# Vision tokenizer and two layers on one core: head matrices later, second norm on GpSimd, running count by products, selection and gather in halves of experts

## The reference

```
def layernorm(y):                       # everywhere, eps = 1e-5
    mu  = mean(y); var = mean((y - mu) ** 2)
    return (y - mu) * rsqrt(var + eps)
# head matrices of the latent attention
core_h = 0.5 * (core + core.T) + head_residual[h] - mean_h(head_residual)
# mixture of experts, expert chooses its tokens
score  = sigmoid(gate_w @ x)            # 8 experts x 384 tokens
top    = the 48 largest scores of each expert
y_e    = layernorm(x)[top] * gamma + beta          # gather
out_e  = fc2_e(gelu(fc1_e(y_e) + b1_e)) + b2_e
x     += scatter of score * out_e back to its tokens
```

## Time and profile before

| | |
|---|---|
| median of 3 runs | 251.8 us (251.53 to 256.31) |
| profiled execution, its own time | 249.22 us |
| its span, first to last instruction | 247.3 us |
| mean granted TensorE clock | 0.984 |
| PE busy | 228.3 us (92%), 1474 instructions |
| DVE busy | 141.3 us (57%) |
| ACT busy | 70.8 us (29%) |
| POOL busy | 63.7 us (26%) |
| fillers, L402 | 156 instructions, 40.2 us busy |

### The profile page before, as it was taken

One profiled execution on the slowest core, in us unless ns is written; L12 is line 12 of the kernel. 1 busy time (PEld: TensorE's weight loads), 2 busy tenths in 40 slices (PEclk: granted clock), 3 DMA queues, 4 the chain that ended last, 5 costly groups with the idle time before them and its releaser, 6 DMA issues.

```text
span 247.3 us, 4034 instructions
## 1 busy us (share of the span) xinstructions
PE 228.3 (92%) x1474; PEld 178.6 (72%) x1474; DVE 141.3 (57%) x401; ACT 70.8 (29%) x176; POOL 63.7 (26%) x146
## 2 busy tenths in 40 slices
PE   6999999999979987999989899999989899999994
PEld 4878788889868876787768678887668554654662
DVE  1657667565667566556665647668479835231212
ACT  2123242275575463125104310313020033120100
POOL 0179941344530150212241402021130340000000
PEclk9999999999999999999999968999999999999999
DMA  6999246920000000299999800000000004782002
GB/s 181 347 415 346 64 107 181 431 96 4 0 0 3 1 3 0 54 420 427 289 343 424 339 0 3 0 0 4 0 0 1 0 3 119 305 360 68 0 3 64
DMA packets 8772, 33.41 MB, mean 135 GB/s; under 512 B 1072, under 2 KB 2864, under 8 KB 6448
## 3 DMA queue, kind: packets, MB, share of 16 engines
q1 hardware_dynamic: 8752, 33.15, 36.7%
HBM read 32.75 MB, written 0.39 MB: 134 GB/s over the span
## 4 chain that ended last, share of the span: by engine, by line
PE 71%; DVE 13%; POOL 4%; DMA 4%; issue 3%; ACT 3%; SPq 1%; DVEq 0%; POOLq 0%
PE bank L411 11%; PE bank L945 6%; PE bank L919 6%; PE bank L642 5%; PE bank L633 5%; PE bank L535 4%; PE bank L402 3%; PE bank L560 3%; PE bank L953 3%; PE bank L513 3%; PE bank L692 2%; DMA bench<-patches 2%; PE bank L892 2%; PE bank L703 2%; PE bank L436 2%
## 5 line engine op out<-in xcount | busy, mean ns | idle before, releaser
L411 PE MATMUL bank<-desk,bench 118*126 118x256 f32 x190 | 43.2, 380 | 1.6 <-DMA desk<-conv_w 1.5
L402 PE MATMUL bank<-zeros 128*128 128x256 f32 x156 | 40.2, 400 | 1.1 <-POOL small L1867 1.1
L411 PEld LDWEIGHTS bank<-desk,bench 118*126 118x126 f32 x190 | 34.8, 188 | 6.9 <-DMA desk<-conv_w 1.9
L402 PEld LDWEIGHTS bank<-zeros 128*128 128x128 f32 x156 | 29.9, 200 | 6.3 <-POOL small L1867 1.1
L1001 DVE TENSOR_REDUCE bench<-bench 118x70 f32<-118x630 f32 x19 | 14.7, 798 | 9.0 <-DMA bench<-patches 9.0
L1637 ACT ACTIVATE attic<-bank,cols 128x126 f32<-128x126 f32 x38 | 15.2, 452 | 12.3 <-PE bank L423 12.1
L1630 ACT ACTIVATE desk<-bank 126x256 f32<-126x256 f32 x19 | 7.3, 383 | 29.1 <-PE bank L411 27.1
L1693 ACT ACTIVATE bench<-bank 128x384 f32<-128x384 f32 x8 | 3.9, 491 | 40.2 <-PE bank L626 40.2
L1874 POOL TENSOR_SCALAR small<-small 96x2 f32<-96x2 f32 (+2 forms) x15 | 3.5, 231 | 43.6 <-DVE small L1212 21.3
L642 PE MATMUL bank<-layw,bench 128*96 128x256 f32 x48 | 13.4, 428 | 1.3 <-ACT bench L1693 0.6
L633 PE MATMUL bank<-bench,layw 128*128 128x192 f32 x72 | 12.9, 332 | 1.5 <-ACT bench L1693 1.4
(11 more groups left out here) (191 smaller groups left out, 420.0 us busy)
## 6 DMA issues: line engine op xcount, KB each, us to landing
attic<-experts SPq DMA_DIRECT2D x10, 1024.0 KB, 8.6
desk<-experts SPq DMA_DIRECT2D x6, 1024.0 KB, 13.6
bench<-patches SPq DMA_DIRECT2D x19, 315.0 KB, 4.3
desk<-tokenizer_w SPq DMA_DIRECT2D x4, 576.0 KB, 6.5
layw<-layer_w SPq DMA_DIRECT2D x1, 2184.0 KB, 11.3
attic<-bias SPq DMA_DIRECT2D x8, 256.0 KB, 12.0
cons<-constants SPq DMA_DIRECT2D x1, 1130.0 KB, 5.3
desk<-conv_w SPq DMA_DIRECT2D x5, 128.0 KB, 3.2
```

The lines of the kernel that those rows point to most:

```text
L402: mm(bank[b][:, 0:C], zeros[:, 0:P], zeros[:, :], start=True, stop=True)
L411: i = mm(conv_bank[t % 2][0:TP, 0:C], xt[t % XRING][0:KP, k, :], convw[0:KP, k, :], start=(k == 0), stop=(k == KX - 1))
```

## The change

It has seven parts.

1. *DMA order at the start.* Each of the five parts of `convw` has a semaphore of its own, and `conv(0)` waits for each in turn; `load_x(1)` comes ahead of the first part of the constants; the head matrices are loaded after `load_x(6)`, and the four parts of `tokw` two tiles later. The first `keep_warm` has 4 products in place of 5.
2. *Head matrices later.* The ten `prepare_heads` stand behind the copies of tiles 5 to 14.
3. *Epsilon in the statistics.* Each statistics buffer has 9 values in place of 6; the last three are set once (24 memsets on DVE) to a third group whose spread adds epsilon to the variance. POOL's addition of epsilon goes everywhere. In `rs_and_shift` the root comes ahead of the negated mean.
4. *Gate values per group.* `halve(0)` and `halve(1)`, 192 columns each, the first ahead of `add_mixed(1)`. Values are turned right after, and ACT copies them out.
5. *Second norm on POOL.* `norm(4, g)` leaves DVE; `norm_again(g)` does it on POOL, ahead of the memset of `ysT`.
6. *Running count by products.* The marked scores are turned at once (4 transposes), the comparison is made on 96 x 32, two dependent additions form sums of whole tiles, and three products with a triangle and with ones give the slot numbers, which one multiplication masks. The scan goes. The filler ahead is 14 products in place of 24, and the fillers of 2 and 2 around the gather go.
7. *Halves.* Picks, weights, gather and the evacuation with gamma and beta run for experts 0 to 3 and then 4 to 7, into banks 2, 3 and 6, 7. POOL's weights wait for all eight half picks. `hidden(q)` waits for its half alone.

Some semaphores of the latent attention are merged, with the same order of work.

```diff
             for k in range(KX):
-                sp.dma_start(convw[:, k, :], convw_d[:, k * C:(k + 1) * C]).then_inc(s("convw_in"), 16)
+                sp.dma_start(convw[:, k, :], convw_d[:, k * C:(k + 1) * C]).then_inc(s(f"convw_in{k}"), 16)
+            load_x(1)
             sp.dma_start(cons[:, 0:CONS_NOW], cons_d[:, 0:CONS_NOW]).then_inc(s("cons_in"), 16)
-            load_x(1)
...
             gate_scores(1)
-            keep_warm(3, 24)
-            pe.wait_ge(s("slots_ready"), 1)
+            pe.wait_ge(s("halved"), G)
             for t in range(TT):
-                pe.transpose(bank[4][0:TR, t * 16:t * 16 + E8], sel8[:, t * TR:(t + 1) * TR], ident[0:E8, 0:E8])
-                i = pe.transpose(bank[4][0:TR, t * 16 + E8:t * 16 + 2 * E8], val8[:, t * TR:(t + 1) * TR],
+                i = pe.transpose(bank[5][0:TR, t * E8:(t + 1) * E8], val8[:, t * TR:(t + 1) * TR], ident[0:E8, 0:E8])
+            i.then_inc(s("vals_turned"), 1)
+            keep_warm(3, 14)
+            pe.wait_ge(s("top"), 2 * TOP_ROUNDS)
+            for t in range(TT):
+                i = pe.transpose(bank[4][0:TR, t * E8:(t + 1) * E8], work8[1][:, t * TR:(t + 1) * TR],
                                  ident[0:E8, 0:E8])
...
+            i.then_inc(s("marks_turned"), 1)
+            pe.wait_ge(s("valT_ready"), 1)
+            pe.wait_ge(s("top"), 2 * TOP_ROUNDS + 1)
+            rank = bank[5][0:TR, 0:TT * E8].rearrange("p (t e) -> p t e", e=E8)
+            mm(rank, upto[0:TR, 0:TR], maskT[0:TR, 0:TT, :], start=True, stop=False, skip_group_check=True)
+            mm(rank[:, 1, :], every[0:TR, 0:TR], maskT[0:TR, 0, :], start=False, stop=False, skip_group_check=True)
+            pe.wait_ge(s("top"), 2 * TOP_ROUNDS + TT - 1)
+            mm(rank[:, 2:TT, :], every[0:TR, 0:TR], maskT[0:TR, TT:, :], start=False, stop=True,
+               skip_group_check=True).then_inc(s("ranked"), 1)
+            pe.wait_ge(s("xh2_ready"), TT)
+
+            def gather(part):
+
+                for t in range(TT):
+                    pe.wait_ge(s("picked"), TT * part + t + 1)
+                    for k in range(KC):
+                        i = mm(bank[gather_bank[part] + k][:, 0:TOK // 2], xh2[0:TR, t, k * P:(k + 1) * P],
+                               pick[0:TR, t, part * HE:(part + 1) * HE, 0:CAP], start=(t == 0), stop=(t == TT - 1))
+                i.then_inc(s("gathered"), 1)
...
-            keep_warm(3, 2)
-            pe.wait_ge(s("ysT_ready"), 2)
+            gather(0)
+            gather(1)
             hidden(0)
...
+                dve.memset(st[:, 6:8], 0.0)
+                dve.memset(st[:, 8:9], EPS * C)
...
-            ts(work8[0], src, 0.0, None, ALU.is_lt).then_inc(s("top"), 1)
-            dve.wait_ge(s("top"), n_top + 1)
-
-            dve.tensor_tensor_scan(work8[1], work8[0], work8[0], 0.0, ALU.add, ALU.max).then_inc(s("top"), 1)
...
+            dve.wait_ge(s("marks_turned"), 1)
+            ts(maskT[0:TR, 0:TT], marks(bank[4]), 0.0, None, ALU.is_lt).then_inc(s("top"), 1)
+
+            for t in range(2, TT):
+                dve.wait_ge(s("top"), 2 * TOP_ROUNDS + t - 1)
+                tt(maskT[0:TR, TT + t - 2, :], maskT[0:TR, (0 if t == 2 else TT + t - 3), :], maskT[0:TR, t - 1, :],
+                   ALU.add).then_inc(s("top"), 1)
+            dve.wait_ge(s("ranked"), 1)
+            tt(slotT[0:TR], marks(bank[5]), maskT[0:TR, 0:TT], ALU.mult).then_inc(s("top"), 1)
+            dve.wait_ge(s("top"), 2 * TOP_ROUNDS + TT)
+            for part in range(2):
+                for t in range(TT):
+                    e = slice(part * HE, (part + 1) * HE)
+                    tt(pick[0:TR, t, e, :], slotT[0:TR, t, e].unsqueeze(2).to_broadcast([TR, HE, SW]),
+                       slots[0:TR].unsqueeze(1).to_broadcast([TR, HE, SW]), ALU.is_equal).then_inc(s("picked"), 1)
...
-            dve.wait_ge(s("wpick_t"), TT)
+            dve.wait_ge(s("weighted"), 2 * TT)
             bias(0)
...
+            def norm_again(g):
+
+                pool.wait_ge(s(f"t_rs_ready{g}"), 5)
+                for n in groups:
+                    pool.wait_ge(s(f"h_ready{n}"), 3)
+                for t in range(TG * g, TG * (g + 1)):
+                    pool.tensor_scalar(xh2[0:TR, t, :], xn[0:TR, t, :], t_mv[0:TR, t, 0:1], t_rs[0:TR, t:t + 1],
+                                       ALU.subtract, ALU.mult).then_inc(s("xh2_ready"), 1)
...
+            pool.wait_ge(s("valT_ready"), 1)
+            pool.wait_ge(s("picked"), 2 * TT)
+            for part in range(2):
+                for t in range(TT):
+                    e = slice(part * HE, (part + 1) * HE)
+                    pool.tensor_tensor(wpick[0:TR, t, e, :], pick[0:TR, t, e, :],
+                                       valT[0:TR, t, e].unsqueeze(2).to_broadcast([TR, HE, SW]), ALU.mult)\
+                        .then_inc(s("weighted"), 1)
```

More of the change, by code:

```diff
@@ L298, in build @@
         mean_m = w_of(cons, CONS, "mean")
+        upto = w_of(cons, CONS, "upto")
+        every = w_of(cons, CONS, "all")
         S = {}
@@ L716, in gate_scores @@
                 i.then_inc(s("gate_done"), 1)
-            keep_warm(7, 5)
-            pe.wait_ge(s("convw_in"), 16 * KX)
+            keep_warm(7, 4)
             conv(0)
@@ L887, in _ @@
-            for g in groups:
-                pe.wait_ge(s(f"xn_ready{g}"), 5 * TG)
-            for t in range(TT):
-                pe.wait_ge(s("pick_t"), t + 1)
-                for k in range(KC):
-                    i = mm(bank[6 + k][:, 0:TOK], xh2[0:TR, t, k * P:(k + 1) * P],
-                           pick[0:TR, t, :, 0:CAP], start=(t == 0), stop=(t == TT - 1))
-            i.then_inc(s("gathered"), 1)
+                i = pe.transpose(bank[5][0:TR, t * E8:(t + 1) * E8], val8[:, t * TR:(t + 1) * TR], ident[0:E8, 0:E8])
@@ L1542, in _ @@
             sum_keys(1, 5)
+            halve(0)
             add_mixed(1)
@@ L1545, in _ @@
             twice_normed(1)
-            dve.wait_ge(s("gate_tanh2"), G)
-            ts(val8, work8[0], 1.0, 0.5, ALU.add, ALU.mult).then_inc(s("top"), 1)
-            n_top = 1
+            halve(1)
             src = val8
-            for r in range(CAP // 8):
-                dve.wait_ge(s("top"), n_top)
+            for r in range(TOP_ROUNDS):
+                dve.wait_ge(s("top" if r else "halved"), 2 * r if r else G)
                 dve.max(m8[:, r, :], src).then_inc(s("top"), 1)
-                if r < G:
-                    norm(4, r, xn, xh2)
-                dve.wait_ge(s("top"), n_top + 1)
+                dve.wait_ge(s("top"), 2 * r + 1)
@@ L2123, in constants @@
         "slots": f(np.tile(np.arange(1, SW + 1), (P, 1))), "spread": f(spread), "heads8": f(heads8),
-        "headcol": f(headcol), "mean": f(np.full((P, P), 1.0 / (C * C)))})
+        "headcol": f(headcol), "mean": f(np.full((P, P), 1.0 / (C * C))), "upto": f(np.triu(np.ones((P, P)))),
+        "all": f(np.ones((P, P)))})
 def kernel(**inputs):
```

158 lines of the change are left out of this document (78 added, 80 removed).

## The result

| | before | changed |
|---|---|---|
| median of 4 runs each | 253.33 us (251.53 to 256.31) | 243.62 us (242.73 to 245.35) |
| profiled execution | 249.22 us, span 247.3 | 242.91 us, span 241.1 |
| mean granted clock in it | 0.984 | 0.977 |

The ratio is 0.965, with a 95% interval of 0.953 to 0.976: 3.5% faster, inside the range and 2.4 us under the predicted 246.0. Between the two profiled executions it is 249.22 - 242.91 = 6.3 us, between the medians 9.7. (Medians here are over all runs of a kernel; the ratios leave disturbed runs out.)

The account below looks back on a forecast made before the run. The prediction took a chain of waits as the bound: nearly all PE from 201.81, DVE before that during ranking. Eight terms summed to 5.75 us, taking the median from 251.8 to 246.0 us; range 243.2 to 250.2.

Parts of the forecast that it names:

- Start: First convolutions: convw waited for part by part and x(1) loaded earlier let conv(1) start near 7.95; gain 0.6 us.
- Heads: First norms: moving the ten head preparation steps behind later copies removes PE's wait at 25.71; gain 0.55 us.
- POOL wait at 89.43: PE's 0.67 us wait for POOL behind rs_local(0): one POOL instruction fewer per rsqrt takes out 0.3 us.
- Norm at 178: Last norm before the gate: negated mean and epsilon leave the front of the power; 0.6 us reaches PE whole.
- Gate values: Halving before the ranking: halve(1) handles 192 columns where halve took 0.80 us over 384; gain 0.45 us.
- Rounds: Ranking rounds on DVE: two norm(4) pairs leave, so two rounds fall from 1.75 to 1.23 us; gain 1.0 us.
- Running count: Between ranking and picks: transposes, comparison, adds and products take 1.65 us where 2.85 was spent; gain 1.2 us.
- Gather: First pick to hidden(0): half picks run alone and the stall goes, 6.05 us in place of 7.1; gain 1.05 us.
- POOL beside DVE: Before the gate: POOL's norms hold up DVE's statistics and halving, losing 0.45 us twice; 246.9 us, chance 0.08.
- The front gives nothing: Early gains of 0.6, 0.55 and 0.3 us end in later waits or fillers; 247.4 us, chance 0.12.
- Weights late: After the picks: POOL's half weightings cost 1.04 us each and end 1.9 us past the limit; 247.9 us, chance 0.06.
- The clock falls: Gather and hidden: fewer ranking fillers leave PE at half speed for 6.76 us, losing 3.4; 249.4 us, chance 0.13.

Follow-up runs that it names:

- the first group: Runs on one chip: the kernel before (253.4 us), the changed kernel again without edit (243.6 us), and variants with front, second norm or running count put back.
- the epsilon variant: Changed kernel with epsilon again added by its own POOL instruction and the negated mean ahead of the root: 246.54 us, 0.963 of the kernel before.
- the second trace of the changed kernel: Changed kernel profiled again with no edit: profiled execution 249.26 us; the median of its timed runs 243.6 us, 0.968 of the kernel before.

## Why the prediction was right, point by point

**Start, 0.6: 0.70.** conv(1) stood at 7.97 where 7.95 was forecast. To hit it so closely is luck: by when the tiles land, turn(0) varies by 1.2 us between traces with this front. And conv(0) ended later than forecast, since four of its products and not two stood behind the last wait for `convw` (6.79); conv(1) had to wait for its tile anyway. **Heads, 0.55: 1.17,** above the upper bound of 0.6. turn(3) waits for nothing, as forecast. What I missed is the second way from a late norm to PE: norm of tile 0, ACT's copy of conv(3), conv(5).

**POOL wait at 89.43, 0.3: 0.** This is the term that failed. It was read from the engine that ended the wait; a second wait, DVE's reciprocal, ends within it. So of the 0.9 forecast for the epsilon the trace shows 0.65.

**Norm at 178, 0.6: 0.61** (2.29 - 1.68, the lead after and before it). **Gate values, 0.45: 0.55.** halve(1) took 0.25. It ran from 180.33 to 180.58, beside the last 0.10 of POOL's first pair of norms and then beside the power; the second pair came from 181.26. Beside POOL's memset it took 0.54 in the variant with the second norm back. The norm on POOL cost 1.22 for each of four, not 0.7: the cover was 2, and nothing waited. It ended at 183.7 against a need at 190. The page "SBUF — State Buffer" of the Trainium skill, section "SBUF: two separate sides", has the loser blocked for a whole instruction, where DVE's instruction has two inputs in SBUF or runs in a two-port mode. By that rule halve(1) might have waited for the norm; it started 0.03 after the tanh it needs had ended (180.30), with the norm still running. The eight picks and products in the variant with weights beside the picks don't bear the rule out either: one after the other they would need 2.77 + 4.63 = 7.40 us, and they took 6.33 (191.26 to 197.59), each side slower (0.35 to 0.66 and 0.58 to 0.72).

**Rounds, 1.0: 1.0.** All six are 1.23. **Running count, 1.2: 1.21** (2.90 - 1.69; the forecast counted the 2.85 before from the start of the compare). **Gather, 1.05: 1.10** (7.1 - 6.00), picks of 0.35 for 0.4. POOL's weights ended 7.55 after the first pick (8.6 forecast, 9.7 the limit).

**The sum.** 0.70 + 1.17 + 0 + 0.61 + 0.55 + 1.0 + 1.21 + 1.10 = 6.3, where 5.75 was forecast, for this execution; the clock took 1.84 of it and gave 1.58 back. Two errors worked against each other here: 0.3 too much at 89.43, 0.6 too little at the head steps. The estimate at full clock from all runs says 7.4. It takes the same 0.45 everywhere, but the fall at 97 cost 1.84 / 6.8 = 0.27 for each us, so I hold 6.3 to 7.4 for what the change takes out. The other 3.4 of the 9.7 us between the medians are the offset: the median of before lay 4.1 above its profiled execution, that of the changed kernel 0.7.

**The offset was the clock.** I added 2.6 us between profiled execution and median as if it were fixed. It is time at 1.2 GHz: before's profiled execution had a clock of 0.984, its median run 0.965 (17.6 us at 1.2 GHz in place of 7.9, by 0.45 that is 4.4 us). The changed kernel's median run has 0.975. Of the 9.8 us between the medians of the first group, 2.4 are this: 0.45 x (17.6 - 12.2).

**Rivals.** POOL beside DVE: no sign. The front gives nothing: true in the profiled execution, where a fall near 97 ate it, false at full clock. Weights late: no. The clock falls: right as a mechanism (no fillers in the ranking: 3.1 us in place, 4.2 us of the median), and a gather at low clock in four of five traces with the changed ranking. 0.13 was too little for it. That the median is low all the same goes with the clock of the whole run, 0.975 where before had 0.965. I priced it 3.4 us for 6.76 us of low clock; the gather went from 5.44 to 8.39 over 6 us of it, 2.95. Slower: no.

## What to carry to other kernels

Price a change where the chain runs, edit by edit, and it adds up; but name a wait's second cause before crediting it, and follow a late result through the buffers that wait for it: the head steps cost PE 0.58 us where it waited and some 0.4 more through a ring. Before a variant's late start is put down to its edit, see whether PE waited for a DMA: the 0.76 us of the epsilon variant were that. Fillers under a stretch in which DVE sets the end are worth their place: without them the ranking and gather took 3.1 us longer. Compare kernels at their granted clocks, or a variant's 6.6 us will be put down to an edit that is worth 1.2.

## What the runs showed of the hardware

The granted clock differs between executions of the same instructions (0.950 to 0.977 for the changed kernel, 0.958 to 0.979 for the one before in the same group), and that difference is most of the spread of their times, at 0.4 to 0.5 us for each us at 1.2 GHz in most kernels. In place it depends on what PE does: 32 products with 32 columns of weights and 128 of data took 2.05 us at full clock before and 2.07 at 1.2 GHz after, the eight products with 32 columns of data 0.99 and 1.78, the gather 5.44 and 8.39. Nearly all falls begin at the same places, behind PE's pauses or narrow products (94 to 98, 141 to 148, 191 to 196; the others at 68.5 in the second trace of the changed kernel, at 184 without fillers, and at the very end of one), and not in every execution: the same pauses stand in traces without the fall. Why one execution has two and another four of them these runs leave open. DVE's picks on 256 columns take 0.35 alone and 0.66 beside POOL; a two-pointer tensor_scalar of 96x256 takes 0.37 on DVE (0.73 for two) and 1.22 on POOL.
